# A mixture-of-experts block: the additions moved behind the last tile, eight late gathers moved ahead of a barrier, and other buffers

## Chip, cores and metric

One core of one Trainium2 chip runs the whole kernel. The metric is the time of one execution on the device in microseconds (us). The profile has the time of one execution of its own. PE is TensorE, DVE is VectorE, ACT is ScalarE, POOL is GpSimd and SP is SyncE; SP issues the large transfers, and POOL issues the gathers (indirect DMAs that fetch 128 rows by a list of indices).

## What is computed

The block takes x of 2048 tokens (2 sequences of 1024) by 256 features and adds three things to it, one after the other: half a feed-forward step, linear attention, and half a feed-forward step again.

```python
x = L0_attn_x
x = x + 0.5 * _L0_ffn_ref(_layernorm(x), gate_weight, w1, w2, w3, sw1, sw2, sw3)
x = x + _L0_attn_ref(_layernorm(x), Wq, Wk, Wv, Wo, Wg1, Wg2, norm_weight)
x = x + 0.5 * _L0_ffn_ref(_layernorm(x), gate_weight, w1, w2, w3, sw1, sw2, sw3)

# _L0_ffn_ref, for each expert e of 32 (a token's weight c is not 0 for its 6 experts alone)
h = silu(x @ w1[e].T) * (x @ w3[e].T)
y = y + c[:, e:e + 1] * (h @ w2[e].T)
# and for all tokens
shared = silu(x @ sw1.T) * (x @ sw3.T) @ sw2.T
return y + shared
```

A token goes to 6 of 32 experts, whose inner width is 128; the shared expert has width 256. All is float32.

## The kernel before, in words

`moe(f, ...)` is a half step, f = 0 the first and f = 1 the second, and `attention(...)` lies between them. Each of the three is a block with a program for each engine, and the engines meet at a barrier at its end (L296 for a half step, L1062 for the attention). A barrier holds a drain of every engine: it takes until what the engine issued is through.

**Pairs.** The tokens of an expert are sorted into tiles of 128 slots, ST = 128 tiles, which are worked through as NQ = 64 pairs. Of these tiles 111 hold tokens with this input; the rest are run as well. For a pair, PE turns the rows and multiplies by w1 and w3 (L911), ACT takes the silu (`gate`, L469), DVE multiplies (L690), PE turns the product (L923), DVE copies it back (L697), PE multiplies by w2 (L931) and ACT copies the result into a result buffer (`output`, L477: `gT` in the first half step, `ey` in the second, RY = 2 buffers for two pairs each). SP stores each buffer into `slot_table` (`store`, L322) and raises `s_there` by 4 tiles once the store before has landed.

**Returned rows.** "Column k" is the k-th of the six results of all tokens; the last tile with a row of it comes earliest for column 5 and latest for column 0. Once the last tile with a row of column k is stored, POOL issues NT = 16 gathers for that column (L420), each of which fetches 128 rows into one of the `returned` buffers. DVE adds each of them to x, weighted (`add_row`, L730), and raises `s_add`. In the first half step POOL fetches the columns 5 and 4 (EARLY = 2, 32 gathers), in the second all six, 5 down to 0 (96 gathers). There are 20 `returned` buffers in the first half step and KEEP = 28 in the second; a gather into a used buffer waits for `s_add`. In the first half step every other gather also waits for `e_h`, the count of pairs that PE has multiplied by w1 and w3. The last EDGE = 8 pairs of both half steps carry four additions each on DVE (`pairs(..., final=True)`), 32 in all.

**Behind the first half step.** POOL waits for all stores, and then fetches the other four columns of two row tiles at once (`gather_rows`, eight gathers, L195), later four for each further row tile. DVE adds them (L1448) and begins the layer norm. PE meanwhile works on what is left of the shared expert (L172, L1137), and then turns the first normed tile (L1148).

**End of the second half step.** SP loads the normed tokens again, 2 MB in one transfer (`again`, L353), after the last pair has been multiplied by w1 and w3. PE runs the shared expert over four groups of 512 tokens (`shared_in`, L817, and `results`, L830), ACT the silu of it, DVE the product (L579) and the addition to x (L669). Between these stand the additions of the columns 3 to 0. Four transfers store the output (L358).

The wait for the buffers, and the pace that the first half step sets, read

```python
if g >= len(returned):
    pool.wait_ge(s_add, g - len(returned) + 1)
if f == 0 and g % 2 == 0:
    pool.wait_ge(e_h, NQ - NT - 3 + g // 2)
```

## Time and profile before

| | us |
|---|---|
| median of three runs | 960.03 |
| the three runs | 955.77, 960.03, 972.37 |
| the profiled execution | 960.5 |
| its span | 958.7 |
| first half step: pairs, from the trace | about 80 to 338 |
| its barrier | 341.8 |
| attention behind it | to 545.8 |
| second half step: pairs | about 604 to 888 |
| from the last pair to the end | to 958.7 |

The execution takes 1.8 us more than its span. Times of the trace count from the span's start. A row of the timeline has the start, the duration, the engine, the line, the operation with its output and input, and in brackets how long the engine had been idle and what ended that. An engine that is idle without need costs nothing; what counts is which wait ends last.

### The profile page before, as it was taken

The numbers are of one execution on the slowest core, as the hardware profiler recorded it, in microseconds if no ns is written. First come the engines' busy times: TensorE is split into PE (matmuls) and PEld (weight loads), VectorE is DVE, ScalarE is ACT, GpSimd is POOL, SyncE is SP. The second block draws the span as 40 slices with busy tenths as digits, with TensorE's granted clock in tenths as the row PEclk, the third lists the DMA queues.
The fourth block names the chain that finished last, engine by engine and source line by source line (L and its number), as shares of the span: only waits on it lengthen the run. The fifth ranks groups of instructions, "written<-read, shape, count | busy, mean of one in ns | idle before, by whom it ended". The sixth has DMA issues, their size and how long they took to land. (4 is left out here: it accounts for less than half of the span.)

```text
span 958.7 us, 16120 instructions
## 1 busy us (share of the span) xinstructions
PE 772.8 (81%) x4554; PEld 609.0 (64%) x4555; DVE 513.0 (54%) x1439; ACT 358.5 (37%) x799; POOL 465.3 (49%) x487
## 2 busy tenths in 40 slices
PE   6895997999969789788889575686999995867486
PEld 6464885888847546576677374564888884645154
DVE  5774942434313537888887469672444431135274
ACT  3160443444424314465665224233444442322000
POOL 3005665553053335867754320655555406456884
PEclk9979898999988898999999755688999998887798
DMA  6862465643233463222220140233444413334524
GB/s 209 338 286 77 158 214 176 231 164 120 89 121 114 159 227 89 80 76 67 72 62 2 34 176 1 77 121 120 153 158 154 138 77 121 126 112 131 207 82 153
DMA packets 42358, 126.43 MB, mean 132 GB/s; under 512 B 8352, under 2 KB 16704, under 8 KB 39488
## 3 DMA queue, kind: packets, MB, share of 16 engines
q1 hardware_dynamic: 23872, 75.40, 20.7%
q0 software_dynamic: 18432, 50.36, 18.0%
q8 instruction: 29, 0.48, 0.2%
q14 instruction: 25, 0.20, 0.1%
HBM read 76.44 MB, written 49.28 MB: 131 GB/s over the span
## 5 line engine op out<-in xcount | busy, mean ns | idle before, releaser
L399 POOL DMA_INDIRECT back<-token_table,slots x192 | 186.7, 973 | 221.9 <-DVE slots L644 96.3
L911 PE MATMUL bank<-w,xt 128*128 x1024 | 260.7, 400 | 33.2 <-ACT xt L492 18.4
L911 PEld LDWEIGHTS bank<-w,xt 128*128 128x128 f32 x1024 | 196.5, 200 | 69.4 <-issue 44.2
L420 POOL DMA_INDIRECT back<-slot_table,combine x124 | 130.0, 1049 | 143.6 <-SPq L328 42.2
L690 DVE TENSOR_TENSOR mids<-mids,bank 128x256 f32<-128x256 f32 x128 | 53.8, 420 | 256.6 <-ACT mids L469 197.3
L931 PE MATMUL bank<-w,mids 128*128 x512 | 142.9, 405 | 4.5 <-DVE mids L697 2.6
L492 ACT COPY xt<-ring 128x256 f32 x256 | 91.5, 408 | 104.0 <-issue 75.9
L931 PEld LDWEIGHTS bank<-w,mids 128*128 128x128 f32 x512 | 93.2, 203 | 16.0 <-issue 7.1
L469 ACT ACTIVATE mids<-bank 128x256 f32<-128x256 f32 x128 | 49.0, 383 | 145.2 <-PE bank L911 87.8
L680 DVE COPY ring<-bank 128x512 f32 (+1 forms) x96 | 66.1, 689 | 46.6 <-PE bank L901 31.2
L923 PE MATMUL bank<-const,mids 128*128 128x128 f32 x256 | 52.6, 290 | 45.7 <-DVE mids L690 24.2
L195 POOL DMA_INDIRECT ring<-slot_table,combine x64 | 64.4, 1006 | 34.9 <-issue 17.4
L923 PEld LDWEIGHTS bank<-const,mids 128*128 128x128 f32 x256 | 36.7, 148 | 63.3 <-issue 29.4
L901 PE MATMUL bank<-const,back 128*128 128x128 f32 x384 | 60.9, 284 | 3.2 <-DMA back<-token_table,slots 3.2
L1111 POOL TENSOR_TENSOR root_a<-power_a,half 128x17 f32<-128x17 f32 (+2 forms) x20 | 51.3, 2564 | 21.1 <-DVE power_a L1465 13.0
L901 PEld LDWEIGHTS bank<-const,back 128*128 128x128 f32 x384 | 50.1, 147 | 14.3 <-DMA back<-token_table,slots 3.4
L477 ACT COPY ey<-bank 128x512 f32<-128x512 f32 x64 | 37.4, 584 | 54.7 <-PE bank L931 31.2
L697 DVE COPY mids<-bank 128x256 f32<-128x256 f32 x128 | 53.4, 417 | 5.7 <-PE bank L923 3.2
L477 ACT COPY gT<-bank 128x512 f32<-128x512 f32 x64 | 37.4, 585 | 49.9 <-PE bank L931 38.3
L730 DVE SCALAR_TENSOR_TENSOR x<-back,share,x 128x256 f32<-128x256 f32 x124 | 50.7, 477 | 4.1 <-DMA back<-slot_table,combine 3.9
L1483 DVE SCALAR_TENSOR_TENSOR ring<-bank,own_a 128x512 f32<-128x512 f32 x64 | 39.7, 683 | 14.4 <-remote 9.6
L817 PE MATMUL bank<-w,sw 128*128 128x512 f32 x64 | 32.0, 659 | 16.9 <-DMA w<-token_columns 12.3
(209 smaller groups left out, 1070.9 us busy)
## 6 DMA issues: line engine op xcount, KB each, us to landing
slot_table<-gT SPq DMA_DIRECT2D x32, 512.0 KB
slot_table<-ey SPq DMA_DIRECT2D x32, 512.0 KB
w<-in_w SPq DMA_DIRECT2D x12, 1024.0 KB, 17.1
slot_table<-w SPq DMA_DIRECT2D x6, 1024.0 KB
token_table<-back SPq DMA_DIRECT2D x8, 512.0 KB, 2.9
back<-token_table,slots POOLq DMA_INDIRECT x192
x<-in_x SPq DMA_DIRECT2D x4, 512.0 KB, 5.7
turn_a<-in_turn SPq DMA_DIRECT2D x4, 512.0 KB
```

What stands on the lines that cost most here:

```text
L195: nc.gpsimd.indirect_dma_start(out=back[j % RB][:, k * H:(k + 1) * H], out_offset=None, in_=y_table, in_offset=bass.IndirectOffsetOnAxis(a ...
L399: pool.indirect_dma_start(out=rows[q % RX][:, a * H:(a + 1) * H], out_offset=None, in_=table, in_offset=bass.IndirectOffsetOnAxis(ap=slots ...
L420: pool.indirect_dma_start(out=returned[g % len(returned)], out_offset=None, in_=y_table, in_offset=bass.IndirectOffsetOnAxis(ap=combine[:, ...
L477: nc.scalar.copy(y[u // 2][:, u % 2 * 2 * H:(u % 2 + 1) * 2 * H], bY[u % 2][:, :]).then_inc(e_y, 1)
L492: last = nc.scalar.copy(xt[u % 2][:, a * H:(a + 1) * H].rearrange("p (k i) -> p k i", k=KC), blocks[:, :, bass.ds(column[a], P)])
L680: last = nc.vector.tensor_copy(blocks[:, :, bass.ds(at, 2 * P)].rearrange("p k (a i) -> p k a i", a=2), new)
L690: nc.vector.tensor_tensor(two(eg[u % 2][:, :]), two(es[u % 2][:, :]), part(u, 1), ALU.mult).then_inc(e_g, 1)
L697: nc.vector.tensor_copy(egT[u % 2][:, :], bG[u % 2][:, 0:2 * P]).then_inc(e_gt, 1)
L901: last = nc.tensor.transpose(bX[u % 2][:, a * H + k * P:a * H + (k + 1) * P], rows[u][:, a * H + k * P:a * H + (k + 1) * P], ident)
L911: last = nc.tensor.matmul(bH[u % 2][:, a * 2 * I:(a + 1) * 2 * I], xt[u % 2][:, a * H + k * P:a * H + (k + 1) * P], w13[:, bass.ds(expert[ ...
L923: last = nc.tensor.transpose(bG[u % 2][:, a * P:(a + 1) * P], eg[u % 2][:, a * I:(a + 1) * I], ident)
L931: last = nc.tensor.matmul(bY[u % 2][:, a * H:(a + 1) * H], egT[u % 2][:, a * I:(a + 1) * I], w2[:, bass.ds(expert[a] * H, H)], start=True, ...
```

## The change

1. **Additions.** All 32 additions that the last eight pairs carried are moved behind the last pair, in both half steps. In the first half step there are 32 buffers for returned rows, partly in space that is free by then, so that no gather waits for an addition; the wait for `e_h` at every other gather goes, and one is left ahead of gather 21. In the second half step there are 20 + 12 + 6 = 38 buffers (space of the first six experts' weights, which POOL waits for at gather 20), and gather 38 is the first that waits for `s_add`. The end of DVE's program there has another order.
2. **Late rows.** The eight gathers of the first two row tiles are issued at the end of the first half step, ahead of the barrier, into a tensor of their own, `first_back`.
3. **Results.** The second half step has four result buffers (RY = 2, 4), and ACT's loop there takes eight pairs a lap.
4. **Shared tokens.** In the second half step SP loads the normed tokens again in four transfers of 512 KB into the ring of tokens, once 56 pairs are through the first product, ahead of the last four stores.
5. **Space.** Some tables share space with others. The lines below count up to 37 higher than before.

```diff
...
+GONE = 6
...
-RY = 2
-RA = 2 * RY
-KEEP = 28
+RY = 2, 4
+KEEP = 20
...
+                    first_back = mem.enter_context(nc.sbuf_tensor("first_back", [P, RB * REST * H], F32))
+                    back = [first_back[:, b * REST * H:(b + 1) * REST * H] for b in range(RB)]
...
-                    returned = [part[:, i * H:(i + 1) * H] for part, n in ((back, NT), (s1, KS * TB // H))
+                    kept, over = sb("kept", [P, H]), (NB % RR + 1) * P + KC * len(LATE) * TB
+                    returned = [part[:, i * H:(i + 1) * H] for part, n in (
+                        (back, NT), (s1, KS * TB // H), (kept, 1), (ring, 4), (ring[:, over:], 2),
+                        (ring[:, SPAN + (NB % RR + 1) * P:], 5)) for i in range(n)]
+                    assert len(returned) >= EARLY * NT
+                else:
+                    y = [sb(f"ey{u}", [P, 4 * H]) for u in range(RY[f])]
+                    products = GONE * WE
+                    s1, *gTs = [w13[:, products + n * KS * TB:products + (n + 1) * KS * TB] for n in range(3)]
...
+                    again = [ring[:, a:a + KC * TB] for a in (spare, spare + KC * TB, SPAN + spare, 0)]
+                    returned = [part[:, i * H:(i + 1) * H] for part, n in ((back, KEEP), (w13, GONE * WE // H), (w2, GONE))
                                 for i in range(n)]
...
+                        turns = NQ // 2 // ry - 4 // ry
...
+                        sp.wait_ge(e_h, done + NQ - EDGE)
                         if f == 0:
-                            sp.wait_ge(e_h, NQ - EDGE)
                             sp.dma_start(area[:, 0:KC * len(LATE) * TB], columns_table[:, 0:KC * len(LATE) * TB]
...
+                        else:
+                            stored = columns_table.rearrange("p (k i t) -> p i k t", k=KC, t=TB)
+                            for it in range(T // TB):
+                                sp.dma_start(again[it].rearrange("p (k t) -> p k t", k=KC), stored[:, it]).then_inc(s_again[it], 16)
...
                         if f == 1:
-                            sp.wait_ge(e_h, done + NQ)
-                            sp.dma_start(again, columns_table).then_inc(s_again, 16)
...
+                                if f == 0 and g == NT + KS * TB // H + 1:
+                                    pool.wait_ge(e_h, NQ - EDGE)
+                                if f == 1 and g == KEEP:
+                                    pool.wait_ge(e_h, done + GONE * NT // 2)
+                                    pool.wait_ge(e_yp, done + GONE * NT // 2)
                                 if g >= len(returned):
                                     pool.wait_ge(s_add, g - len(returned) + 1)
-                                if f == 0 and g % 2 == 0:
-                                    pool.wait_ge(e_h, NQ - NT - 3 + g // 2)
                                 pool.indirect_dma_start(
                                     out=returned[g % len(returned)], out_offset=None, in_=y_table,
                                     in_offset=bass.IndirectOffsetOnAxis(
                                         ap=combine[:, i * TOPK + k:i * TOPK + k + 1], axis=0)
                                 ).then_inc(s_back[n] if n < TOPK - 1 else s_last[i // 4], 16)
+                        if f == 0:
+                            pool.wait_ge(s_share, 1)
+                            pool.wait_ge(s_there, ST + 4)
+                            for j in range(RB):
+                                gather_rows(j, j)
...
-                        def add_row(n, i):
...
                                 dve.wait_ge(s_back[n], NT * 16)
                             else:
                                 dve.wait_ge(s_last[i // 4], NT // 4 * 16)
-                            if n:
-                                dve.wait_ge(s_add, g - NT + 1)
-                            if f == 0:
-                                dve.wait_ge(s_yc, 2 * len(its))
-                            elif n > 3:
-                                dve.wait_ge(s_yc, 2 if n == 4 else 4 if i < NT // 2 else 8)
+                            if begun(before):
+                                dve.wait_ge(s_add, before)
+                            if begun(shared):
+                                dve.wait_ge(s_yc, shared)
...
-                                if final:
-                                    for g in range(i * 2 * NT // n, (i + 1) * 2 * NT // n):
-                                        add_row(g // NT, g % NT)

...
+                        dve.sem_inc(s_share, 1)
...
-                        with dve.Fori(0, (NQ - EDGE - NP) // 2) as it:
+                        with dve.Fori(0, (NQ - NP) // 2 - 1) as it:
                             pairs(it * 2 + NP, 2)
-                        pairs(NQ - EDGE, EDGE, final=True)
+                        pairs(NQ - 2, 2)
                         copy_mid(NQ - 1, NQ - 1)
-                        if f == 1:
-                            def add_rows(n, a=0, b=NT):
+                        if f == 0:
+                            for n in range(EARLY):
+                                for i in range(NT):
+                                    add_row(n, i, (n - 1) * NT + i + 1, 2 * len(its))
+                        else:
+                            def add_rows(n, shared, a=0, b=NT):
                                 for i in range(a, b):
...
+                                    add_row(n, i, (n - 1) * NT + i + 1, shared)
+
...
-                            add_rows(2)
+                            add_rows(0, 0)
                             product(0)
-                            add_rows(3)
+                            add_rows(1, 0)
                             product(1)
-                            dve.wait_ge(s_add, 4 * NT)
-                            shared_of(0, 2)
-                            add_rows(4)
+                            shared_of(0, 2, 2)
+                            add_rows(2, 2)
                             product(2)
-                            dve.wait_ge(s_add, 5 * NT)
-                            shared_of(2, 4)
+                            shared_of(2, 4, 3)
                             product(3)
-                            add_rows(5, 0, NT // 2)
-                            shared_of(4, 8)
-                            add_rows(5, NT // 2, NT)
+                            add_rows(3, 4)
+                            shared_of(4, 8, 4)
+                            add_rows(4, 8)
+                            add_rows(5, 8)
...
+                                pe.wait_ge(s_again[it], 16)
...
-                            pe.wait_ge(s_again, 16)
-                            shared_in(0, again)
...
-                        pool.wait_ge(all_there, ST + 4)
-                        for j in range(RB):
-                            gather_rows(j, j % B)
```

POOL at the end of the first half step and behind its barrier, before (L420 are gathers of returned rows, L296 the barrier, L195 the late rows, `e_h` and `s_add_0` as above):

```order
L420 DMA back<-slot_table,combine 128x256 [waits e_h,s_add_0]
L420 DMA back<-slot_table,combine 128x256 [waits s_add_0]
L296 UNCONDITIONAL_BRANCH
L1089 UNCONDITIONAL_BRANCH [waits barrier_Pool_Activation_PE_DVE_SP_gather]
L195 DMA ring<-slot_table,combine 128x256 [waits s_there_0]
L195 DMA ring<-slot_table,combine 128x256 x7
L1111 TENSOR_TENSOR root_a<-power_a,half 128x1 [waits a_var]
L195 DMA ring<-slot_table,combine 128x256 [waits a_add]
```

The same place now; L434, L307 and L197 are those three lines, and L1135 is the line L1111 of before:

```order
L434 DMA kept<-slot_table,combine 128x256
L434 DMA ring<-slot_table,combine 128x256 [waits e_h]
L434 DMA ring<-slot_table,combine 128x256 x10
L197 DMA first_back<-slot_table,combine 128x256 [waits s_there_0,s_share_0]
L197 DMA first_back<-slot_table,combine 128x256 x7
L307 UNCONDITIONAL_BRANCH
L1113 UNCONDITIONAL_BRANCH [waits barrier_Pool_Activation_PE_DVE_SP_gather]
L1135 TENSOR_TENSOR root_a<-power_a,half 128x1 [waits a_var]
L197 DMA first_back<-slot_table,combine 128x256 [waits a_add]
L197 DMA first_back<-slot_table,combine 128x256 x3
```

The gathers of column 4 have one wait for `e_h` and none for additions, and the eight gathers of late rows stand ahead of the barrier.

DVE at the end of the pairs of the second half step, before (L690 and L697 are a pair's two steps, L730 the additions, L579 and L669 the shared expert; `s_back2_1` is the landing of the third column):

```order
L697 COPY mids<-bank 128x256 [waits e_yp,e_gp]
L730 SCALAR_TENSOR_TENSOR x<-back,share,x 128x256 [waits s_add_1,s_back1_1] x4
L697 COPY mids<-bank 128x256 [waits e_yp,e_gp]
L730 SCALAR_TENSOR_TENSOR x<-back,share,x 128x256 [waits s_add_1,s_back2_1] x16
L579 TENSOR_TENSOR w<-w,bank 128x512 [waits s_si_1]
L579 TENSOR_TENSOR w<-w,bank 128x512
L730 SCALAR_TENSOR_TENSOR x<-back,share,x 128x256 [waits s_add_1,s_back3_1] x16
L579 TENSOR_TENSOR w<-w,bank 128x512 [waits s_si_1]
L579 TENSOR_TENSOR w<-w,bank 128x512
L669 SCALAR_TENSOR_TENSOR x<-bank,x 128x512 [waits s_y_1,s_add_1]
L669 SCALAR_TENSOR_TENSOR x<-bank,x 128x512 [waits s_y_1]
L730 SCALAR_TENSOR_TENSOR x<-back,share,x 128x256 [waits s_yc_1,s_add_1,s_back4_1] x16
```

The same place now, where these lines are L710, L717, L748, L599 and L689:

```order
L717 COPY mids<-bank 128x256 [waits e_yp,e_gp] x2
L748 SCALAR_TENSOR_TENSOR x<-back,share,x 128x256 [waits s_back0_1] x16
L599 TENSOR_TENSOR w<-w,bank 128x512 [waits s_si_1]
L599 TENSOR_TENSOR w<-w,bank 128x512
L748 SCALAR_TENSOR_TENSOR x<-back,share,x 128x256 [waits s_add_1,s_back1_1] x4
L748 SCALAR_TENSOR_TENSOR x<-w,share,x 128x256 [waits s_add_1,s_back1_1] x12
L599 TENSOR_TENSOR w<-w,bank 128x512 [waits s_si_1]
L599 TENSOR_TENSOR w<-w,bank 128x512
L689 SCALAR_TENSOR_TENSOR x<-bank,x 128x512 [waits s_y_1,s_add_1]
L689 SCALAR_TENSOR_TENSOR x<-bank,x 128x512 [waits s_y_1]
L748 SCALAR_TENSOR_TENSOR x<-w,share,x 128x256 [waits s_yc_1,s_add_1,s_back2_1] x6
L748 SCALAR_TENSOR_TENSOR x<-back,share,x 128x256 [waits s_yc_1,s_add_1,s_back2_1] x10
```

No addition stands between the pairs, the first column's sixteen additions follow the last pair, and the whole second column's follow the first product of the shared expert.

## Rows read from the trace of the kernel before

**Rows 1.** The page, part 1: busy time of each engine over the span.

```profile
PE 772.8 (81%) x4554; PEld 609.0 (64%) x4555; DVE 513.0 (54%) x1439; ACT 358.5 (37%) x799; POOL 465.3 (49%) x487
```

**Rows 2.** Windows of the second half step: us, then busy time per engine, clock, DMA share, GB/s.

```profile
790.00:886.00 96.00, 65.82 (x252) 50.74 (x251) 26.31 (x69) 26.48 (x68) 53.16 (x55) 0.83 0.38 122
886.00:959.00 73.00, 47.57 (x134) 26.34 (x132) 35.91 (x82) 5.52 (x10) 49.93 (x42) 0.85 0.46 149
```

**Rows 3.** Timeline of POOL, second end: start, duration, engine, line, tiles, [idle before <-releaser].

```profile
790.80 0.96 POOL L420 DMA_INDIRECT back<-slot_table,combine  x1 [30.40 <-SPq L328]
...
809.77 0.96 POOL L420 DMA_INDIRECT back<-slot_table,combine  x1 [0.30 <-issue]
...
882.85 0.96 POOL L420 DMA_INDIRECT back<-slot_table,combine  x1 [3.79 <-DVE x L730]
...
888.27 5.24 POOL L420 DMA_INDIRECT back<-slot_table,combine  x1 [0.30 <-issue]
...
947.20 1.22 POOL L420 DMA_INDIRECT back<-slot_table,combine  x1 [0.30 <-issue]
```

**Rows 4.** Timeline of ACT, second end, last pairs.

```profile
807.19 0.59 ACT L477 COPY ey<-bank 128x512 f32<-128x512 f32 x1 [8.10 <-remote]
...
813.48 0.38 ACT L469 ACTIVATE mids<-bank 128x256 f32<-128x256 f32 x1 [5.09 <-PE bank L911]
...
834.99 0.59 ACT L477 COPY ey<-bank 128x512 f32<-128x512 f32 x1 [5.29 <-remote]
...
840.64 0.38 ACT L469 ACTIVATE mids<-bank 128x256 f32<-128x256 f32 x1 [4.45 <-PE bank L911]
...
862.15 0.38 ACT L469 ACTIVATE mids<-bank 128x256 f32<-128x256 f32 x1 [6.55 <-remote]
...
881.01 0.39 ACT L469 ACTIVATE mids<-bank 128x256 f32<-128x256 f32 x1 [8.68 <-remote]
```

**Rows 5.** Timeline of DVE, second end: last copy of a pair, train of additions.

```profile
885.93 0.42 DVE L697 COPY mids<-bank 128x256 f32<-128x256 f32 x1
886.26 6.41 DVE L730 SCALAR_TENSOR_TENSOR x<-back,share,x 128x256 f32<-128x256 f32 x16
```

**Rows 6.** Timeline of PE, second end: first matmuls of the shared tokens.

```profile
900.16 9.08 PE L817 MATMUL bank<-w,sw 128*128 128x512 f32 x16 [12.29 <-DMA w<-token_columns]
```

**Rows 7.** Drains at the barriers: count, duration ns min/median/max, first and last start.

```profile
L296 POOLq DRAIN  x2: 6118/16418/26717, 323.0 to 930.7; - x2
...
L296 DVEq EVENT_SEMAPHORE  x2: 21/21/21, 341.8 to 958.6; - x2
...
L1062 POOLq DRAIN  x1: 8229/8229/8229, 537.5 to 537.5; - x1
```

**Rows 8.** Timeline of POOL, first end and the attention behind it.

```profile
307.81 0.95 POOL L420 DMA_INDIRECT back<-slot_table,combine  x1 [9.87 <-DVE x L730]
...
324.03 1.19 POOL L420 DMA_INDIRECT back<-slot_table,combine  x1 [0.30 <-DVE x L730]
...
342.55 0.95 POOL L195 DMA_INDIRECT ring<-slot_table,combine  x1 [17.33 <-POOLq L296]
...
351.32 0.95 POOL L195 DMA_INDIRECT ring<-slot_table,combine  x1 [0.30 <-issue]
```

**Rows 9.** Timeline of ACT, first end.

```profile
281.14 0.38 ACT L469 ACTIVATE mids<-bank 128x256 f32<-128x256 f32 x1 [7.87 <-remote]
...
322.04 0.38 ACT L469 ACTIVATE mids<-bank 128x256 f32<-128x256 f32 x1 [5.86 <-remote]
```

**Rows 10.** Timeline of DVE, first end and the attention behind it.

```profile
336.50 0.41 DVE L697 COPY mids<-bank 128x256 f32<-128x256 f32 x1
...
354.57 2.04 DVE L1448 SCALAR_TENSOR_TENSOR x<-ring,share,x 128x256 f32<-128x256 f32 x4 [7.57 <-DMA ring<-slot_table,combine]
```

**Rows 11.** Timeline of PE behind the barrier.

```profile
352.31 3.62 PE L1137 MATMUL bank<-sw,ring 128*128 128x256 f32 x16
359.02 0.69 PE L1148 MATMUL bank<-const,ring 128*128 128x128 f32 x2 [3.10 <-ACT ring L1330]
```

111 lines of the change are left out of this document (57 added, 54 removed).

## The prediction

> **What bounds the kernel now.** I read first the page's busy times: PE is busy for 81% of the span and POOL for 49% [rows 1], so over most of the kernel PE sets the pace. Then I read windows of the second half step, because an average hides the ends: PE is busy 65.82 of 96 us in the last pairs and 47.57 of 73 us behind them [rows 2]. Neither is full. The timelines of these stretches say what is.
>
> At the second end POOL is the limit. Its gathers are 18.97 us for 15 intervals, 1.265 us apart (790.80 to 809.77), and from 882.85 on they never stop until the last starts at 947.20 [rows 3]. The span ends at 958.7, 11.5 us behind that. There are 44 of them, so 43 intervals take 64.35 us where 43 x 1.265 = 54.4 would do: 10.0 us are pauses. One is plain to see: the gather at 888.27 takes 5.24 us instead of 0.96 [rows 3] and ends at 893.5, soon after the train of additions that DVE runs from 886.26 to 892.67 [rows 5]. In the last pairs before that ACT is held six times, for 8.10, 5.09, 5.29, 4.45, 6.55 and 8.68 us [rows 4]; each lies in, or ends within 3 us of, a row of gathers on POOL, the first two those from 790.80 to 810.7 [rows 3].
>
> At the first end the pairs finish (last copy 336.50 [rows 10]), the stores land, and the barrier falls at 341.8 [rows 7]. POOL had issued its last gather at 324.03 [rows 8] and its drain of 6.12 us was long over [rows 7]. Behind the barrier DVE waits 7.57 us for the late rows, until 354.57 [rows 10]; PE is busy with shared products until 355.93 and then waits 3.10 us for the first normed tile, at 359.02 [rows 11].
>
> **First half step: the pairs.** The 32 additions leave the last eight pairs. ACT's two long holds, 7.87 us at 281.14 and 5.86 us at 322.04 [rows 9], lie beside gathers, and the gathers stay: 32 before, 32 now. Those for column 4 still come in a row of eleven, from the pair that `e_h` names. So I take 0 for the pairs, the last copy at about 337; the bounds are a hold more or less, -6 to +6 us, by those two rows.
>
> **First half step: the barrier.** This is the first big term. DVE now has 32 additions to do behind the last copy, at 6.41 / 16 = 0.40 us each [rows 5]: 12.8 us, 337 to 349.7. POOL wakes when all stores have landed, which is what lets the barrier fall before, and issues the eight late gathers from about 342.2. Without disturbance the last starts 8.77 us later, as before (342.55 to 351.32 [rows 8]): 351.0. Beside additions a gather has been held until the train ends [rows 3, 5]: then two or three are issued by 345, one is held to 349.9, and the last starts at about 356. I take 356, since the train and the gathers now start together. Behind it the drain must end. The shortest that I can read is 324.03 + 5.1 (the drain of 6.12 us that began at 323.0 ended at 329.2), the longest 947.20 + 10.3 (26.72 us from 930.7) [rows 3, 7, 8]. I take the short one, 5.1: this barrier is the same as that first one, and few gathers are in flight. The barrier falls at 361 instead of 341.8: **+19.2**, with bounds 356.1 (+14.3) and 366.3 (+24.5). Before, this drain cost nothing because the last pairs covered it; that cover is gone.
>
> What comes back: the rows are there at the barrier, so DVE doesn't wait its 7.57 us. But PE's shared work from 341.93 to 355.93 isn't moved and takes its 14 us after the barrier, and the first normed tile can be used no sooner. So of the 17.2 us from barrier to 359.02 only the 3.10 us of PE's wait go [rows 11]; later tiles might keep up to the 7.57 us [rows 10]. I take -3.5, bounds -1 and -7.5. The sum of the first half step: 19.2 - 3.5 = **+15.7**, bounds +7 (14.3 - 7.5) and +23.5 (24.5 - 1).
>
> **Second half step: the pairs.** With 38 buffers POOL issues 16 gathers of column 5 and then 22 of columns 4 and 3 before it must wait for an addition; before it was 16, 12 and twice 12. By the rows, a row of 16 (20 us) held ACT for 8.10 + 5.09 = 13.2 us, a row of 12 (15 us) for 5.29 + 4.45 = 9.7, then 6.55 and 8.68 [rows 4]: about its length less 6 us. A row of 22 lasts 27.8 us and would hold for 21.8, in place of 9.74 + 6.55 + 8.68 = 25.0, and the shorter waits of the fourth row of about 2 us go as well. The last copy comes at 881 instead of 885.93 [rows 5]: -5, bounds -12 (the 22 break into two rows, which hold less) and +4 (they hold for their whole length).
>
> **Second half step: behind the pairs.** This is the second big term. No addition is made before 881, so POOL stands at gather 38 until 881.8, and 58 gathers are left instead of 44. 57 x 1.265 = 72.1 us. The pauses: five trains of sixteen additions (columns 5 to 1) now lie beside gathers, where three did. The first costs what the one at 886.26 did, 4.5 us; the 5.5 us that are left of the 10.0 came with the other two, 2.7 each, so 4.5 + 4 x 2.7 = 15.3. The last gather starts at 881.8 + 72.1 + 15.3 = 969.2, and the end comes 11.5 us behind it as before: 980.7 instead of 958.7, **+22.0**. Low: 874 + 72.1 + 10.0 + 11.5 = 967.6 (+9). High: 890.8 + 72.1 + 5 x 4.5 + 11.5 = 996.9 (+38).
>
> The shared tokens come earlier, and PE's 12.29 us of waiting at 900.16 go [rows 6]. I cost that at 0: the shared products then end some 17 us before POOL's gathers do, and the end waits for POOL. It would be worth up to 12.3 us if POOL's chain weren't the later one. The four loads stand on SP's queue ahead of the last four stores, which hold tiles behind the 111 that matter; 0. The additions wait behind a product of the shared expert (rows of column 4 behind product 0, at about 881 + 14): POOL may go to gather 53 on the sixteen additions of column 5, which takes it until 906, so it isn't stopped; 0. Four result buffers take away a wait of ACT's copies, if there was one; 0, since gates (L469), which need no result buffer, are held as long as copies [rows 4]. The order of loads, tables and the weights' place: 0.
>
> **Sum.** 960.5 + 15.7 + 22.0 = **998.2** us, made against the profiled execution, 960.5, which lies 0.5 from the median of 960.03. I predict 998.
>
> **A rule against this change.** The gather at 888.27 took 5.24 us and ended with the train of additions beside it [rows 3, 5]. The Trainium skill, page "SBUF — State Buffer", section "Who interferes with whom", has a rule for this: an instruction of VectorE with two inputs in SBUF and one of GpSimd that reads SBUF take one pair of ports, and the second blocks until the first is through. The trace agrees in part: most gathers beside a train keep to 0.96 to 1.25 us, and one in each train is stretched. By the rule in full no gather would pass a train, and the kernel would take some 1015 us; by the rows it is 998.
>
> **Rivals.**
>
> *The holds on ACT are waits for result buffers or for additions, and go (faster side).* ACT's copies at 807.19 and 834.99 are held 8.10 and 5.29 us [rows 4]; with four buffers and free of additions all six holds, 38 us, might go in the second half step. The last copy would come at 848 and the end at 848.8 + 72.1 + 15.3 + 11.5 = 947.7, -11; with the first half step's +15.7 that makes 965. If the holds of the first half step go too (13.7 us [rows 9]), it is 951. The point is whether a copy or gate is still held beside sixteen gathers. Against it: at 807 no addition had run yet, and gates are held as well.
>
> *The second half step's tail costs little.* The trains don't slow gathers where the landing paces them (10 us of pauses in all), the 22 gathers break in two, and the late rows go through undisturbed: 960.5 + 7 + 9 = 977, up to 985.
>
> *Additions block gathers altogether.* The gather at 888.27 waited for its train's end [rows 3, 5]; if every train holds POOL for its whole length, the five cost 5 x 6.41 = 32 us instead of 15.3, and the sum is 998.2 + 16.7 = 1015. With a row of 22 that holds the pairs for its full length and a drain of 10.3 us both bounds together give 960.5 + 23.5 + 38 = 1022. The other gathers beside trains, at 1.2 us or less for most, speak against it: all pauses together are 10.0 us.
>
> *The late rows do no harm, and the barrier isn't later than DVE's additions.* Then the first half step is 349.7 + 0.3 against 341.8, +8 - 3.5: the sum is 987.
>
> **Chances.** Near the forecast (985 to 1010, with the last rival) 0.57; the cheap tail (970 to 985) 0.15; holds gone in the second half step only (about 965) 0.10; gone in both (about 951 or less) 0.08; worse (above 1010) 0.10. 80% of this lies between 962 and 1016. A difference of under 2% of 960 (941 to 979) is about what a measurement here can't tell from no change. Faster by over 2% needs more than the best rival gives, 0.05; within 2% has most of both rivals on holds and part of the cheap tail, 0.22; slower 0.73.
>
> **What would show it.** In the profile after: POOL's eight late gathers between 342 and 357, one of them stretched, the barrier at 356 to 366, and PE's first transpose of the attention some 14 us behind it; in the second half step ACT still held beside the gathers, the last copy at about 881, 58 gathers without a wait behind it, and the last at 960 to 975, with PE and the shared expert done well before. The forecast is wrong if ACT is no longer held at the ends, if the barrier falls with DVE's last addition, or if gathers come closer together than 1.26 us.

## The result, and the profile after

The changed kernel takes 998.25 us (median of four runs, 996.69 to 998.97) against 964.57 us for the kernel before (four runs, 955.77 to 972.37). The ratio is 1.0379, with a 95% interval of 1.0286 to 1.0471: slower by 3.8%. The profiled execution took 998.04 us, its span is 996.2 us against 958.7.

The barrier of the first half step first. The view of the barrier's line and the two that follow have the columns of [rows 7], [rows 8], [rows 10] and [rows 11]:

```profile
L307 DVEq EVENT_SEMAPHORE  x2: 21/21/21, 367.4 to 996.2; - x2
```

```profile
346.01 7.93 POOL L197 DMA_INDIRECT first_back<-slot_table,combine  x1 [27.14 <-SPq L363]
354.25 0.94 POOL L197 DMA_INDIRECT first_back<-slot_table,combine  x1 [0.30 <-issue]
...
361.76 0.95 POOL L197 DMA_INDIRECT first_back<-slot_table,combine  x1 [0.30 <-issue]
```

```profile
340.03 0.43 DVE L717 COPY mids<-bank 128x256 f32<-128x256 f32 x1 [0.20 <-PE bank L948]
340.37 6.41 DVE L748 SCALAR_TENSOR_TENSOR x<-back,share,x 128x256 f32<-128x256 f32 x16
...
348.68 4.44 DVE L748 SCALAR_TENSOR_TENSOR x<-ring,share,x 128x256 f32<-128x256 f32 x11
...
375.17 2.04 DVE L1469 SCALAR_TENSOR_TENSOR x<-first_back,share,x 128x256 f32<-128x256 f32 x4
```

```profile
367.49 13.24 PE L173 MATMUL bank<-ring,sw 128*128 128x512 f32 x24 [22.10 <-PEq L307]
...
380.57 3.62 PE L1158 MATMUL bank<-sw,ring 128*128 128x256 f32 x16
384.02 0.38 PE L1169 MATMUL bank<-const,ring 128*128 128x128 f32 x2
```

The last copy of a pair is at 340.03 (336.50 before [rows 10]), and the barrier falls at 367.4 instead of 341.8 [rows 7]. What lies between is the two steps that were moved there, one behind the other. POOL wakes at 346.01, 5.6 us into the additions, and its first gather takes 7.93 us, to 353.94, while DVE's last addition ends at 353.12. The other seven follow 1.25 us apart, the last at 361.76, and 5.6 us later the barrier falls. Behind the barrier DVE has its rows without waiting (375.17; before, it waited 7.57 us [rows 10]), but PE is busy with shared products until about 384 and makes the first transpose at 384.02, 16.6 us behind the barrier; it was 17.2 [rows 7, 11]. So the first tile gains only 0.6 us. The shared products themselves had become slower. Before the change their first 24 matmuls read

```profile
341.93 10.54 PE L172 MATMUL bank<-ring,sw 128*128 128x512 f32 x24 [0.32 <-PEq L296]
```

and now they take 13.24 us, 2.7 more. PE had stood idle for 22.10 us ahead of them, and the granted clock was 0.51 from 367 to 373, about the lower of its two levels, where it was 1.00 from 341.9 to 347 before the change. The same 24 matmuls take 13.13 us behind 8.05 us of idling in the run with the eight gathers behind the barrier (below), and 10.54 behind 0.33 us with both moves undone.

The second end, with the columns of [rows 3], and then ACT's holds as in [rows 4]:

```profile
865.52 0.96 POOL L434 DMA_INDIRECT w<-slot_table,combine  x1 [0.30 <-issue]
897.21 0.96 POOL L434 DMA_INDIRECT back<-slot_table,combine  x1 [30.73 <-DVE x L748]
...
900.05 3.65 POOL L434 DMA_INDIRECT back<-slot_table,combine  x1 [0.30 <-DVE x L748]
...
968.07 4.84 POOL L434 DMA_INDIRECT back<-slot_table,combine  x1 [0.30 <-DVE x L748]
...
986.01 0.96 POOL L434 DMA_INDIRECT back<-slot_table,combine  x1 [0.30 <-DVE x L748]
```

```profile
824.89 0.59 ACT L496 COPY ey<-bank 128x512 f32<-128x512 f32 x1 [6.63 <-remote]
...
830.47 0.38 ACT L488 ACTIVATE mids<-bank 128x256 f32<-128x256 f32 x1 [4.38 <-PE bank L936]
...
848.84 0.59 ACT L496 COPY ey<-bank 128x512 f32<-128x512 f32 x1 [4.25 <-PE bank L956]
...
860.10 0.38 ACT L488 ACTIVATE mids<-bank 128x256 f32<-128x256 f32 x1 [10.06 <-remote]
...
869.95 0.59 ACT L496 COPY ey<-bank 128x512 f32<-128x512 f32 x1 [9.47 <-remote]
```

```profile
896.12 0.42 DVE L717 COPY mids<-bank 128x256 f32<-128x256 f32 x1 [0.20 <-PE bank L948]
```

```profile
897.89 7.03 PE L842 MATMUL bank<-ring,sw 128*128 128x512 f32 x16
```

POOL issues 38 gathers by 866.5, stands 30.73 us until the first addition, and then has 58 left, without a wait of its own: 88.8 us from 897.21 to 986.01, of which 57 x 1.265 = 72.1 are the gathers themselves and 16.7 are pauses. In each of the five trains of additions (a train is sixteen additions in a row) one gather is stretched, to between 3.26 and 4.84 us; the first and the last stand above. The span ends 10.2 us behind the last gather's start. Before, 44 gathers were left from 882.85 on [rows 3], 41 of them behind the last copy. ACT's five long holds, 34.8 us together, lie beside the rows of 16 and 22 gathers, as the six of before did [rows 4]. In the longest of them ACT's silu waits for these matmuls:

```profile
850.35 3.21 PE L936 MATMUL bank<-w,xt 128*128 x8 [2.29 <-ACT xt L511]
```

They end at 853.56 (the ends of matmuls are modelled), and the silu starts at 860.10, 6.5 us later. It also waits for DVE's product of the pair before, but DVE has been idle all that time. So PE's answer reaches ACT late, while POOL issues one gather after another. The shared expert starts right behind the last pair, at 897.89, without the 12.29 us of [rows 6], and this gives nothing back.

### The profile page after: what moved, and what is told of

It is laid out like the page before. It is cut to its first block and busy times, and to the rows that moved or that the text cites. A ratio compares the mean times of both kernels' runs of the same rounds, so it can differ in the third digit from the quotient of the medians.

```text
span 996.2 us, 16058 instructions
## 1 busy us (share of the span) xinstructions
PE 764.8 (77%) x4554; PEld 605.6 (61%) x4555; DVE 514.0 (52%) x1439; ACT 358.4 (36%) x799; POOL 476.2 (48%) x487
## 5 line engine op out<-in xcount | busy, mean ns | idle before, releaser
L710 DVE TENSOR_TENSOR mids<-mids,bank 128x256 f32<-128x256 f32 x128 | 53.8, 420 | 274.7 <-ACT mids L488 218.9
L434 POOL DMA_INDIRECT back<-slot_table,combine x76 | 86.7, 1140 | 129.6 <-SPq L336 75.7
L956 PE MATMUL bank<-w,mids 128*128 x512 | 140.7, 400 | 7.5 <-issue 4.9
L956 PEld LDWEIGHTS bank<-w,mids 128*128 128x128 f32 x512 | 92.0, 200 | 18.7 <-issue 10.4
L197 POOL DMA_INDIRECT first_back<-slot_table,combine x64 | 71.6, 1118 | 44.8 <-SPq L363 27.1
L1135 POOL TENSOR_TENSOR root_a<-power_a,half 128x17 f32<-128x17 f32 (+2 forms) x20 | 51.2, 2562 | 33.1 <-DVE power_a L1486 25.0
L717 DVE COPY mids<-bank 128x256 f32<-128x256 f32 x128 | 53.5, 418 | 10.0 <-remote 4.4
L496 ACT COPY gT<-bank 128x512 f32<-128x512 f32 x64 | 37.4, 584 | 53.8 <-PE bank L956 37.5
L842 PE MATMUL bank<-ring,sw 128*128 128x512 f32 x96 | 47.5, 653 | 5.8 <-DVE gT L599 3.2
L434 POOL DMA_INDIRECT w<-slot_table,combine x36 | 37.3, 1036 | 11.0 <-issue 10.7
## 6 DMA issues: line engine op xcount, KB each, us to landing
w<-in_w SPq DMA_DIRECT2D x12, 1024.0 KB, 17.2
```

Of the source, the lines that this page charges most:

```text
L197: nc.gpsimd.indirect_dma_start(out=back[j % RB][:, k * H:(k + 1) * H], out_offset=None, in_=y_table, in_offset=bass.IndirectOffsetOnAxis(a ...
L434: pool.indirect_dma_start(out=returned[g % len(returned)], out_offset=None, in_=y_table, in_offset=bass.IndirectOffsetOnAxis(ap=combine[:, ...
L496: nc.scalar.copy(y[u // 2][:, u % 2 * 2 * H:(u % 2 + 1) * 2 * H], bY[u % 2][:, :]).then_inc(e_y, 1)
L710: nc.vector.tensor_tensor(two(eg[u % 2][:, :]), two(es[u % 2][:, :]), part(u, 1), ALU.mult).then_inc(e_g, 1)
L842: last = nc.tensor.matmul(bS[m][:, :], sw13[:, k * 2 * SI + m * P:k * 2 * SI + (m + 1) * P], tokens[k], start=(k == 0), stop=(k == KC - 1))
L956: last = nc.tensor.matmul(bY[u % 2][:, a * H:(a + 1) * H], egT[u % 2][:, a * I:(a + 1) * I], w2[:, bass.ds(expert[a] * H, H)], start=True, ...
```

## Experiments

Each kernel is the changed one with the edit shown. Ratios are to the kernel before on the same chip, with 95% intervals. The twelve runs came in three groups, and each group ran on another chip: in the first the kernel before took 962.9 us, in the second 971.71, in the third 883.8. So times are compared within a group, and across groups by ratio. The changed kernel itself ran in none of the three groups, and its chip isn't recorded. Where its trace is set beside one of theirs, it is by the distance between two events in each, and the places of the last copies scatter by several us between traces.

### First half step: the eight late gathers behind the barrier again

```diff
-                        if f == 0:
-                            pool.wait_ge(s_share, 1)
-                            pool.wait_ge(s_there, ST + 4)
-                            for j in range(RB):
-                                gather_rows(j, j)
...
+                        for j in range(RB):
+                            gather_rows(j, j)
                         for j in range(RB - 5, NT + 2):
                             roots(j - 1)
```

> The changed kernel with one part undone: the eight late gathers stand behind the barrier again. My theory (the gathers ahead of the barrier are held by the train of additions and then put their landing and POOL's drain on the way to the barrier): the barrier falls with the last addition, at about 353.5 us instead of 367.4; the rows are late again by some 12.8 us behind it, of which the attention gives back about 4; the time is about 988 to 990, 9 less than the changed kernel. Rival 1 (moving them ahead hides them, the barrier is late for DVE's additions alone): the time rises by 3 to 8, to above 1001. Rival 2 (it doesn't matter): 998.

Measured: 986.36 us, ratio 1.0232 [1.0190, 1.0274]. The barrier falls at 348.6, with the last addition, 13.4 us behind the last copy (335.25) where it was 27.4:

```profile
L307 DVEq EVENT_SEMAPHORE  x2: 21/21/21, 348.6 to 986.4; - x2
```

```profile
335.25 0.42 DVE L712 COPY mids<-bank 128x256 f32<-128x256 f32 x1 [0.19 <-PE bank L942]
...
343.90 4.44 DVE L743 SCALAR_TENSOR_TENSOR x<-ring,share,x 128x256 f32<-128x256 f32 x11
```

The gathers ahead of the barrier cost 1.5%, some 14 us, more than the 9 that I expected. The traces agree: 14.0 us between last copy and barrier, of which the attention, 201.3 us here and 200.0 in the changed kernel, gives back only 1.3, not 4. The rival, that the early gathers hide something, is out.

### First half step: the additions back in the last eight pairs

```diff
-                        with dve.Fori(0, (NQ - NP) // 2 - 1) as it:
+                        inside = f == 0
+                        last = EDGE if inside else 2
+                        with dve.Fori(0, (NQ - last - NP) // 2) as it:
                             pairs(it * 2 + NP, 2)
-                        pairs(NQ - 2, 2)
+                        pairs(NQ - last, last, final=inside)
```

> The changed kernel with the first half step's 32 additions back in its last eight pairs; the eight late gathers stay ahead of the barrier. My theory: no gather is stretched (0.95 us each), the eight run from about 346 to 355, and the barrier falls some 5.5 us later, at about 360 instead of 367.4; the time is about 991. Rival (the additions in the pairs delay the last copy by what they take, 13 us): the barrier isn't earlier and the time is 998 or more.

Measured: 990.65 us, ratio 1.0274 [1.0228, 1.0321]. The timeline of POOL has the eight gathers at their usual length, and the barrier at 358.7:

```profile
344.32 0.94 POOL L197 DMA_INDIRECT first_back<-slot_table,combine  x1 [25.15 <-SPq L363]
...
353.05 0.94 POOL L197 DMA_INDIRECT first_back<-slot_table,combine  x1 [0.30 <-issue]
```

```profile
L307 DVEq EVENT_SEMAPHORE  x2: 21/21/21, 358.7 to 994.2; - x2
```

The last gather starts at 353.05, and the barrier follows 5.6 us later, as in the changed kernel. With no train beside them no gather is stretched. The last copy, at 338.59, isn't later for carrying the additions.

The profiled execution took 996.08 us, 5.4 more than the median, and the end of its trace shows something that the others don't:

```profile
923.27 7.03 PE L847 MATMUL bank<-ring,sw 128*128 128x512 f32 x16
...
956.89 0.95 POOL L434 DMA_INDIRECT back<-slot_table,combine  x1 [0.30 <-issue]
...
959.51 1.09 ACT L464 ACTIVATE w<-bank 128x512 f32<-128x512 f32 x2 [38.41 <-remote]
```

From 920.36 to 956.89 POOL issues 30 gathers in one row without a pause. The matmuls that this silu needs end at 930.30, and the silu starts 29.2 us later, 1.7 us after the last gather of the row has ended.

### First half step: both undone

> The changed kernel with both of these undone: additions back in the last eight pairs of the first half step and the eight late gathers behind the barrier; the buffers and the second half step stay changed. My theory: the first half step's loss of about 21 us goes, the barrier falls at about 345 (341.8 in the kernel before), and the time is 976 to 979. Rival (the loss in the first half step comes from the gathers that aren't paced any more or from the shared space, which both stay): 985 or more.

Measured: 980.03 us, ratio 1.0169 [1.0120, 1.0218]. The barrier is at 341.6 (341.8 before the change), the attention ends at 543.7 (545.9 before, 567.4 in the changed kernel). The time is slightly above the 976 to 979 that I expected, and well below the rival's 985. So the first half step's loss is these two moves and nothing else of the change, and 1.7% is left for the second half step.

### Second half step: the additions back in the last eight pairs

The same edit as above with `inside = f == 1`, and the first two `add_rows` behind the pairs taken out.

> The changed kernel with the second half step's 32 additions back in its last eight pairs, and its 38 buffers kept. My theory (the end is POOL's row of gathers, and each gather that can't be issued before the last pair costs 1.265 us): POOL starts again at the first of these pairs, about 38 to 44 gathers are left behind the last copy instead of 58, and the end comes 15 to 25 us sooner: 973 to 983. Rival (the additions cost the pairs as much as they free, through longer holds on ACT): 992 or more.

Measured: 1002.29 us, ratio 1.0411 [1.0356, 1.0466]: nothing gained, as the rival had it. POOL did start again at the 56th pair, but two things took the gain. The last copy moved from 896.12 to 918.80, as 29 more gathers ran ahead of it (29 are left behind it, for 58), and 32 additions. And then POOL stood for 21.97 us:

```profile
944.68 0.96 POOL L434 DMA_INDIRECT w<-slot_table,combine  x1 [21.97 <-DVE x L748]
```

```profile
918.80 0.42 DVE L717 COPY mids<-bank 128x256 f32<-128x256 f32 x1
...
940.75 1.28 DVE L599 TENSOR_TENSOR w<-w,bank 128x512 f32<-128x512 f32 x2 [10.10 <-ACT w L464]
...
943.92 2.46 DVE L748 SCALAR_TENSOR_TENSOR x<-w,share,x 128x256 f32<-128x256 f32 x6
```

The gather at 944.68 needs a buffer whose addition (943.92) is queued on DVE behind two products of the shared expert. The order that the change gives to DVE's end doesn't suit a POOL that has come as far as this.

### The same with DVE's order of before

```diff
+                            add_rows(2, 0)
                             product(0)
+                            add_rows(3, 0)
                             product(1)
-                            shared_of(0, 2, 2)
-                            add_rows(2, 2)
+                            shared_of(0, 2, 4)
+                            add_rows(4, 2)
```

> As the run with the second half step's additions back in its last eight pairs, but DVE's program behind the last pair has the order of the kernel before (additions of column 3 ahead of the first product of the shared expert, of column 2 ahead of the second). In that run POOL stood 21.97 us at gather 70, for additions that were queued behind the shared expert's product, and the last copy came 22.7 us later than in the changed kernel. If it was that order that kept the gain back, POOL now runs on from about 922 with 26 gathers left: 26 x 1.265 + 10 us of pauses + 10 us to the end, some 976 us of span, 20 less than the changed kernel. If a gather ahead of the last copy costs the pairs as much as it saves behind it, the time is 992 or more.

Measured: 986.72 us, ratio 1.0190 [1.0126, 1.0255]; the span of its profile is 980.2 us. The last copy is at 921.95 and the end 58.3 us behind it, where the changed kernel has 896.12 and 100.1. So of 41.8 us that fewer gathers and fewer trains behind the last pair are worth, the pairs take 25.8 back. ACT's holds of over 3 us come to 52.8 us there, for 34.8 in the changed kernel, which is 18.0 of the 25.8. The run before it lost what was left through the order.

### Second half step: gathers in twos

```diff
+                                if f == 1 and g < len(returned) and g % 2 == 0:
+                                    pool.wait_ge(e_h, done + 45 + g // 2)
```

> The changed kernel, and in the second half step every other one of the first 38 gathers waits for one more pair (e_h), so that they come in twos instead of rows of 16 and 22. Theory 1 (ACT's holds come from long rows of gathers, because the answers of TensorE reach the others only in the gaps): the holds of 6.63, 4.38, 4.25, 10.06 and 9.47 us go, the last copy comes 15 to 35 us sooner than 896, the 58 gathers behind it are the same, and the time is 965 to 985. Theory 2 (each gather costs the pairs its time however they come): 995 to 1002. Theory 3 (the holds are additions or result buffers): no change, 998; no additions run there and there are four buffers already.

Measured: 970.01 us, ratio 1.0014 [0.9969, 1.0060], with a span of 966.7 us for 996.2. POOL's gathers now come in groups of one to six, and of ACT's holds (34.8 us in the changed kernel) two of about 3 us are left:

```profile
822.37 0.95 POOL L436 DMA_INDIRECT back<-slot_table,combine  x1 [1.53 <-remote]
823.62 0.95 POOL L436 DMA_INDIRECT back<-slot_table,combine  x1 [0.30 <-issue]
827.50 0.95 POOL L436 DMA_INDIRECT back<-slot_table,combine  x1 [2.92 <-PE bank L938]
828.76 0.95 POOL L436 DMA_INDIRECT back<-slot_table,combine  x1 [0.30 <-issue]
```

```profile
818.47 0.38 ACT L490 ACTIVATE mids<-bank 128x256 f32<-128x256 f32 x1 [3.08 <-PE bank L938]
...
822.12 0.58 ACT L498 COPY ey<-bank 128x512 f32<-128x512 f32 x1 [3.27 <-PE bank L958]
```

```profile
869.57 0.42 DVE L719 COPY mids<-bank 128x256 f32<-128x256 f32 x1 [0.20 <-PE bank L950]
```

The last copy is at 869.57, 26.6 us sooner. The 58 gathers behind it are the same, but one of the five trains stretches none of them, and from the last copy to the end it is 97.1 us instead of 100.1. Theory 1 holds on this chip, and theories 2 and 3 don't.

### The additions with one input

```diff
-                            nc.vector.scalar_tensor_tensor(
-                                x[:, i * H:(i + 1) * H], returned[g % len(returned)], share[:, i * TOPK + k:i * TOPK + k + 1],
-                                x[:, i * H:(i + 1) * H], ALU.mult, ALU.add).then_inc(s_add, 1)
+                                nc.vector.tensor_scalar(
+                                    x[:, i * H:(i + 1) * H], returned[g % len(returned)], share[:, i * TOPK + k:i * TOPK + k + 1],
+                                    None, ALU.mult).then_inc(s_add, 1)
```

> The changed kernel, in which the second half step's additions are left out: in their place DVE multiplies the returned rows by their weight into x, so with one input in the memory instead of two (the sum isn't made). If it is the second input that holds POOL's gathers, the pauses of 16.7 us between the 58 gathers go and the time is some 17 us shorter, 981. If any work of DVE of that size does it, or the semaphores that it raises, it is 998; if such a product takes the ports for itself, more than that.

Measured: 1002.12 us, ratio 1.0358 [1.0310, 1.0405]; not faster. But the pauses are gone:

```profile
897.96 1.09 POOL L434 DMA_INDIRECT back<-slot_table,combine  x1 [31.52 <-DVE x L753]
...
937.23 0.95 POOL L434 DMA_INDIRECT w<-slot_table,combine  x1 [0.30 <-issue]
944.65 1.08 POOL L434 DMA_INDIRECT w<-slot_table,combine  x1 [6.47 <-DVE x L753]
```

```profile
897.35 4.86 DVE L753 TENSOR_SCALAR x<-back,share 128x256 f32<-128x256 f32 x16
...
941.80 0.69 DVE L689 SCALAR_TENSOR_TENSOR x<-bank,x 128x512 f32<-128x512 f32 x1 [16.58 <-remote]
```

```profile
922.83 1.08 ACT L464 ACTIVATE w<-bank 128x512 f32<-128x512 f32 x2 [15.90 <-remote]
943.36 1.09 ACT L464 ACTIVATE w<-bank 128x512 f32<-128x512 f32 x2 [19.44 <-remote]
```

From 897.96 to 937.23 are 32 gathers in 39.27 us, 1.267 us apart, though two trains of DVE lie beside them. So no gather is stretched beside work with one input. That this is for the input and not for the shorter train (4.86 us for 6.41) isn't told apart by this run. What took the 17 us is a new wait: in a row of 32 gathers without a pause TensorE's answers reach ACT late in the shared expert too (15.90 and 19.44 us before two silus, 9 to 10 in the changed kernel), DVE waits 16.58 us, and POOL 6.47 us for DVE; and the end comes 20.6 us behind the last gather (976.34) instead of 10.2, for the work that had fallen behind. It looks as if the pauses had let those answers through, and the 38.41 us of the run above, in a row of 30 gathers with the real additions, point the same way. No run tests it by itself.

### Two result buffers

```diff
-RY = 2, 4
+RY = 2, 2
```

> The changed kernel with two result buffers again in the second half step, and ACT's laps of four pairs. Mine (no wait of ACT is for a result buffer): 998, within 1.5 us. Rival (the 11.3 us by which the last copy of the second half step lies closer to the attention's end than before came from the four buffers): 1003 to 1009.

Measured: 1006.32 us, where the rival was: 1003 to 1009. But the ratio is 1.0414 [1.0339, 1.0488], and this overlaps with the changed kernel's. The two profiles agree up to the attention's end (567.4 in both) and behind the last copy (99.9 and 100.1 us to the end), and the last copy is at 904.78 instead of 896.12, 8.7 us later. Part of that is scatter. From the attention's end to the last copy it is 337.4 us here, and in five traces with four buffers and the same pairs it is 328.7 (the changed kernel), 330.4 (the run with one input, on this chip), 331.7, 333.5 and 337.0 (the first group). Against the trace on the same chip that is 7.0 us for two buffers, with a scatter as large as that.

### On a third chip: both halves, the pacing of the first, additions in the pairs, and two buffers

The third group combined them. `paced_undone` is the paced kernel with the first half step's two moves undone; `both_paced` also has

```diff
-                                if f == 1 and g < len(returned) and g % 2 == 0:
-                                    pool.wait_ge(e_h, done + 45 + g // 2)
+                                if g < len(returned) and g % 2 == 0:
+                                    pool.wait_ge(e_h, done + (45 if f else 49) + g // 2)
```

and in the first half step column 5's additions in the last four pairs and column 4's behind them; `paced_pairs` adds the second half step's additions in the pairs with the order of before; `paced_two` is the paced kernel with two result buffers.

> The changed kernel with the gathers of the second half step in twos (the run paced) and the first half step's two moves undone (the run first_undone). If the two causes are independent, the time is that of the run paced less some 18 to 21 us, so 0.98 of the kernel before. If the holds and the barrier share one cause, less is gained, 0.99 or more.

> As paced_undone, and in the first half step too every other gather waits for one more pair, from the 49th on; column 5's additions lie in the last four pairs, column 4's behind the last. Theory 1 (ACT's holds there, 9.33 + 6.74 + 7.95 us in the changed kernel, come from long rows of gathers): most of these 24 us go, the additions behind the last pair give back some 4, and the time is 10 to 20 us below paced_undone. Rival (in the first half step something else holds ACT, and column 4's additions behind the last pair now cost): the same or up to 6 us more than paced_undone.

> As both_paced, and the second half step's 32 additions are back in its last eight pairs, with DVE's order of before behind them. Without long rows the additions cost the pairs nothing, and three trains lie beside POOL's gathers instead of five: some 5 us of pauses less, so 5 us below both_paced. If additions in the pairs hold the pairs, or let POOL run in long rows again: 0 to 15 us above it.

> The run paced with two result buffers in the second half step instead of four. If more result buffers only help where ACT is held by long rows of gathers: the same as the run paced within 2 us (1.00 of before). If they help by themselves, or it is ACT's longer lap: 5 to 9 us more, 1.008 of before.

| kernel | us | ratio | 95% interval |
|---|---|---|---|
| before | 883.8 | 1 | |
| paced_undone | 882.57 | 1.0000 | 0.9976 to 1.0024 |
| both_paced | 884.81 | 1.0006 | 0.9989 to 1.0023 |
| paced_pairs | 876.7 | 0.9927 | 0.9897 to 0.9958 |
| paced_two | 902.18 | 1.0210 | 1.0172 to 1.0247 |

`paced_undone` was expected at 0.98 and came at 1.0000, and `paced_two` at 1.00 to 1.008 and came at 1.0210; both expectations took over gains from the other two chips that aren't there on this one. Whether the two causes add up is not answered by it.

On this chip the kernel before takes 8% less than on the others, and the traces say why: ACT isn't held. The first half step is the same program in `first_undone` (first chip) and in `paced_undone` (this chip). From the 25th to the 33rd pair's copy on DVE it takes 27.37 and 27.36 us, with a granted clock of 1.00 in both (200 to 250 us). From the 49th to the 57th, beside the row of gathers, it takes 40.86 us on the first chip and 25.92 on this one (clock from 250 to 300: 0.83 and 1.00). The attention is shorter there as well, 196.7 us for 202.1; why is open. The timeline of POOL in the first half step of `paced_undone`, which has no pacing there:

```profile
251.24 0.94 POOL L436 DMA_INDIRECT back<-slot_table,combine  x1 [35.98 <-SPq L336]
...
290.68 0.95 POOL L436 DMA_INDIRECT ring<-slot_table,combine  x1 [0.30 <-issue]
```

These are 32 gathers without a gap, and between 251 and 307 ACT is nowhere idle for 3 us or more, where a row of 16 cost 13 to 16 us on the other chips. So `both_paced` had nothing to gain, and gained nothing; the 10 to 20 us of its theory 1 were for a chip with holds. `paced_pairs` is 0.7% faster than the kernel before, 8 us below `both_paced` where I had expected 5. `paced_two` is 19.6 us above `paced_undone`: by the traces, its attention ends at 516.9 instead of 504.1, 12.8 us, for the two moves of the first half step (with both paced alike in the second). From there to the last copy it takes 284.2 us instead of 279.3 (279.4 in `both_paced`), 4.9 more for two buffers. And from the last copy to the end it is 99.9 us instead of 96.1, because in `paced_undone` two of the five trains stretch no gather. The timeline of ACT shows a part of the 4.9. These are the first copies (L508, L513) of two groups of four pairs that follow each other, in `paced_undone` and then in `paced_two`:

```profile
657.63 0.71 ACT L508 COPY xt<-ring 128x256 f32 x2 [2.65 <-issue]
...
670.86 0.72 ACT L508 COPY xt<-ring 128x256 f32 x2 [2.18 <-PE bank L937]
```

```profile
672.28 0.71 ACT L513 COPY xt<-ring 128x256 f32 x2 [2.65 <-issue]
...
685.98 0.71 ACT L513 COPY xt<-ring 128x256 f32 x2 [2.65 <-issue]
```

Inside a lap of eight pairs the second group comes 13.23 us behind the first, and from lap to lap of four it is 13.70 us. So a lap of eight saves some 0.47 us per eight pairs where nothing else disturbs, about 3 of the 4.9 us over the half step. Another 2.3 us are a wait for a result buffer itself, in `paced_two` alone, at its last pairs, where the four loads of shared tokens stand ahead of the last stores on SP's queue:

```profile
799.25 0.58 ACT L498 COPY ey<-bank 128x512 f32<-128x512 f32 x1 [2.31 <-DMA slot_table<-ey]
```

I haven't run the longer lap without the buffers.

## Why the prediction was right, and where it was not

The time was forecast at 998 and came at 998.25. The two large terms, the barrier and the tail of gathers, work as forecast, but that the sum is so close is luck: two errors of over 6 us cancel. The times that the forecast gave for the second half step are on the clock of the kernel before; with the 15.7 us of the first half step its last copy would be at 897 (measured 896.12) and its last gather at 985 (986.01).

- **First half step, the pairs: 0.** The last copy came at 340.03 instead of 336.50. The runs with the same pairs there and no additions in them have it at 335.25 to 341.23, so this is scatter.
- **The barrier: +19.2 forecast, +25.6 measured.** Right: the train and the gathers start together, one gather is held to the end of the train, and the drain is the short one (5.6 us from the last start, taken as 5.1). Mis-sized, and 1.1 us outside its own bounds: I let two or three gathers through before the hold and had the last at 356; POOL woke at 346.0, later than my 342.2, and the first gather was the one that was held, so the last started at 361.76. Of the 6.4 us, 3.0 are the later last copy (340.03 for 337), and 3.4 are the hold and the drain.
- **What comes back: -3.5 forecast, -4.1 measured** (barrier to the attention's end, 204.1 us before and 200.0 after). The size is right and the way is not: I took the 3.10 us of PE's wait for the first tile, and the first tile gained 0.6. I had kept the shared work at 14 us; behind PE's 22 us of idling it took 16.7 at the lower clock. The rest came with later tiles.
- **Second half step, the pairs: -5 forecast, -11.3 measured** (attention's end to last copy, 340.0 and 328.7 us). The holds were sized well: 35.0 us forecast (13.2 and 21.8), 34.8 measured, for 38.1 before. The term that failed is the 0 for four result buffers. They are worth 4.9 us on the third chip. Here about 3 us are theirs, by the longer lap on ACT: from the 25th to the 33rd pair's copy it is 27.41 us before and 26.98 after, where no additions run. The holds give 3.3 of the 5 that I took for them, and the 5 us that are left are within the scatter of this stretch: four other traces with the same pairs have 330.4 to 337.0 us.
- **Behind the pairs: +27 forecast (99.7 us from last copy to end), 100.1 measured,** against 72.8 before: 58 gathers at 1.265 us, 16.7 us of pauses for 15.3, and 10.2 for 11.5 to the end. The run with both of the first half step's moves undone has 100.1 us there too.
- **The shared tokens: 0,** as measured: the shared expert is through at 943.9 and POOL 42 us later.

Together +25.6 - 4.1 - 11.3 + 27.3 = +37.5 us between the spans; the errors of the barrier (+6.4) and of the pairs (-6.3) cancel.

**The rival on ACT's holds** was wrong: with sixteen gathers in a row ACT was still held, with four buffers and no addition near. The paced run shows what holds it on that chip: long rows of gathers. That they do this on two chips and not on the third is shown; what in the chip makes the difference is open. With it stays open how much the unchanged second half step would lose or gain on the third chip from the change's 17 additional gathers behind the last copy (58 for 41): the kernel before left no trace there.

**The rule on the ports.** A train with two inputs stretches at most one gather, and a train with one input stretches none (the run with one input). In six of the nine traces with five trains at the end, each of the five stretches one; in `paced` four do, in `paced_undone` three, in `first_pairs` two. The Trainium skill, page "SBUF — State Buffer", section "Who interferes with whom", says that a VectorE instruction with two inputs in SBUF contends with one of GpSimd that reads SBUF. The traces agree in so far as a gather is stretched beside such additions alone. But the rule is about one instruction, and a train is sixteen of 0.40 us each. The forecast's reading of it, that no gather would pass a train, was an extension, the 1015 of the rival, and wrong by 17 us: most gathers beside a train pass at 0.96 to 1.28 us. Why one of them waits for the end of the whole train, and why in some trains none does, stays open.

## What to carry to other kernels

A step that overlaps with the last tiles can cost nothing there and its whole length behind them: before moving it behind the loop, ask which engine's queue starts later for it, and what that engine then has left (here 58 gathers for 41). A transfer ahead of a barrier isn't hidden by the barrier; it makes the barrier wait for its landing, and for whatever its engine is blocked by on the way. On two of three chips here gathers were best issued a few at a time between the steps that they would delay, and a gain or loss that comes from such delays should be measured on more than one chip.

## What the runs showed of the hardware

- The same kernel takes 962.9, 971.7 and 883.8 us on three chips. On the first two, ACT stands idle for 4 to 14 us at a time beside rows of 16 to 22 gathers, though TensorE's matmuls have ended (up to 10.4 us ago: they end at 277.01 and the silu starts at 287.45 in `paced`); on the third a row of 32 gathers passes without a hold of 3 us.
- One gather in a train of additions is stretched to 3.3 to 7.9 us, in most trains but not in all; with a product of one input in the additions' place none is.
- These pauses may not be all loss: without them, waits of 15 to 19 us for TensorE's answers appeared elsewhere (the run with one input), and one of 38.41 us beside 30 gathers in a row (`first_pairs`).
- TensorE's 24 matmuls of 128x512 take 10.54 us behind 0.3 us of idling, at a granted clock of 1.00, and 12.5 to 13.2 us behind 8 to 22 us of idling (0.51 in the first 6 us of the changed kernel's).
- A lap of eight pairs instead of four on ACT saves 0.4 to 0.5 us per eight pairs.
